# A decoder of six sublayers on one core: the mixture and the recurrence joined to the first attention, two norms in one factor

## The reference: what is computed

```python
x = _layernorm(x + _L0_attn_ref(x, ...))           # window attention, 16 heads; token 0 attends over all
x = _layernorm(x + _L0_xattn_ref(x, ctx_512, ...)) # causal attention plus cross attention, one output weight
x = _layernorm(x + _L0_ffn_ref(x, ...))            # mixture: each of 16 experts takes its 64 best tokens
x = _layernorm(x + _L1_attn_ref(x, ...))           # gated linear recurrence, then a gated MLP
x = _layernorm(x + _L1_xattn_ref(x, ctx_512, ctx_512, ...))
x = _layernorm(x + _L1_ffn_ref(x, ...))            # top 2 of 8 experts
```

## Time and profile before

| | us |
|---|---|
| median of three runs | 590.47 |
| lowest, highest | 588.93, 591.81 |
| the profiled execution | 588.99 |
| its span in the trace | 587.3 |
| first attention, to the last normed rows | 0 to 266.9 |
| mixture | 267.2 to 359.4 |
| recurrence and MLP | 359.9 to 417.8 |
| second attention with the top-2 mixture | 418.1 to the end |

### The profile page before, as it was taken

How to read it: one execution, slowest core, us unless ns; L and a number is a source line. 1 busy time by engine, 2 the same in 40 slices (tenths; PEclk the granted TensorE clock), 3 DMA queues, 4 the chain that set the end, 5 groups by cost and what they waited for, 6 DMA issues and landing times. The chain is left out here.

```text
span 587.3 us, 10442 instructions
## 1 busy us (share of the span) xinstructions
PE 478.7 (82%) x3790; PEld 233.6 (40%) x3837; DVE 381.4 (65%) x876; ACT 222.9 (38%) x449; POOL 181.0 (31%) x296
## 2 busy tenths in 40 slices
PE   3899999978879889875079994697599888999994
PEld 2445444433334333332037992246333333444441
DVE  7454766877667686515996557954458875466474
ACT  2303444454746646651002102432202666724221
POOL 6651639457363370406200004300142400000000
PEclk9899999999989999997589997989599999999998
DMA  7230103055411120006212004000031200060700
GB/s 233 67 81 27 47 2 103 19 172 173 138 55 27 49 56 4 3 1 226 98 53 93 3 2 160 1 2 1 26 89 48 57 3 3 33 184 1 215 19 18
DMA packets 26899, 38.03 MB, mean 65 GB/s; under 512 B 3648, under 2 KB 19520, under 8 KB 26464
## 3 DMA queue, kind: packets, MB, share of 16 engines
q1 hardware_dynamic: 26848, 37.36, 21.0%
HBM read 23.91 MB, written 0.59 MB: 42 GB/s over the span
## 5 line engine op out<-in xcount | busy, mean ns | idle before, releaser
L1070 DVE TENSOR_REDUCE nmax<-bank 128x2 f32<-128x512 f32 (+2 forms) x240 | 144.9, 625 | 79.8 <-PE bank L844 34.1
L956 ACT ACTIVATE arena<-bank 128x512 f32<-128x512 f32 (+2 forms) x256 | 130.7, 526 | 121.7 <-PE bank L848 84.4
L502 PE MATMUL bank<-causal_qk,identb 128*128 128x512 bf16 x255 | 80.8, 418 | 33.6 <-DVE moe_top L1350 16.0
L844 PE MATMUL bank<-arena 62*128 62x256 bf16 (+2 forms) x512 | 86.0, 257 | 12.9 <-DVE nmax L1070 5.3
L848 PE MATMUL bank<-arena 64*128 64x256 bf16 (+2 forms) x512 | 85.6, 256 | 2.2 <-ACT arena L956 1.5
L889 PE MATMUL bank<-arena 128*32 128x256 f32 (+4 forms) x1088 | 72.8, 346 | 8.6 <-ACT arena L956 3.7
L844 PEld LDWEIGHTS bank<-arena 62*128 62x128 bf16 x512 | 29.9, 94 | 79.3 <-issue 46.0
L502 PEld LDWEIGHTS bank<-causal_qk,identb 128*128 128x128 bf16 x298 | 26.4, 105 | 68.4 <-issue 40.0
L714 POOL TENSOR_SCALAR_AFFINE_SELECT arena<-arena 128x256 f32<-128x256 f32 x64 | 25.5, 407 | 48.6 <-ACT arena L956 47.8
L848 PEld LDWEIGHTS bank<-arena 64*128 64x128 bf16 x512 | 30.3, 94 | 16.5 <-issue 6.9
L889 PEld LDWEIGHTS bank<-arena 128*32 128x32 f32 x1088 | 21.4, 109 | 33.7 <-issue 18.6
(11 more groups left out here) (284 smaller groups left out, 794.5 us busy)
## 6 DMA issues: line engine op xcount, KB each, us to landing
arena<-arena SPq DMA_DIRECT2D x96, 128.0 KB, 2.4
fcw<-in_fc1T SPq DMA_DIRECT2D x16, 256.0 KB, 3.3
arena<-in_fc2T SPq DMA_DIRECT2D x1, 4096.0 KB, 14.9
arena<-comb_rows SPq DMA_DIRECT2D x16, 256.0 KB, 4.7
fcw<-in_last SPq DMA_DIRECT2D x1, 2304.0 KB, 8.3
arena<-pos_rows SPq DMA_DIRECT2D x16, 128.0 KB, 3.0
arena<-comb_rows SPq DMA_DIRECT2D x16, 128.0 KB, 4.5
w<-in_w SPq DMA_DIRECT2D x1, 1216.0 KB, 6.1
```

The source lines that it names most:

```text
L502: nc.tensor.matmul(bank[:, :], m.identb[:, :], m.causal_qk[:, 0:4, :], start=True, stop=True)
L844: mins = t.matmul(mout[:, i, :], stack_rows(m, nm, h0 + i, 0, MAX_ROWS)[:, qt * P:(qt + 1) * P], stack_rows(m, nm, h0 + i, 1, MAX_ROWS)[:, ...
L956: s.activation(m.prob[h % 8][:, 0:w], score_bank(n, h)[:, 0:w], ACT.Exp).then_inc(exps, 1)
L1070: v.tensor_reduce(m.nmax[n % 2][:, qt, h0:h0 + nh], MX[c % NMX][:, 0:nh * (k1 - k0)].rearrange("p (h k) -> p h k", h=nh), AX.X, ALU.max, n ...
```

## The change

Mixture and recurrence have no block of their own any more. `expert_choice` is now a side part of the first attention's pipeline and its `then`, which makes `LAST` the last job's table of steps instead of `FAR`; `recurrence` is called from it. The parts:

1. Every `cross` job that norms a sequence computes a second factor on GpSimd, (1 + eps) * var + 1e-5 * eps (`scaled_variance`), the power is taken for both at once (4 columns instead of 2), and DVE writes the rows twice: first as the mixture wants them (`m.x[1]`), then as before (`m.x[2]`). Squares, sums and the scaling of all rows at the mixture's start are gone.
2. Router, biases are loaded at slot 140, `fc2` behind the last value product. `norm_weight`'s transpose is at slot 226. Tiles 0 to 5 (three sequences) are transposed, weighed and multiplied by the router in slots 230 to 241, in the drain of the last job; only tiles 6 and 7 go through this chain after the last norm. GpSimd's constants are made at slot 230.
3. The scattered rows get x2 by 8 float32 matmuls with the identity, placed ahead of the scattering, in place of DVE's addition. Statistics and norms are made on pairs of tiles and read the banks. The norm's factor is that of layer norm and root mean square in one (`m.rms`); the rows with the layer norm alone, which the residual needs, are made from it on GpSimd (`rows_back`).
4. The large memset of the value buffers goes from DVE to GpSimd, the small ones behind the first `residual`.
5. The layer norm of tiles 4 to 7 at the end of the recurrence leaves the block: `LastNorm` makes it in the first slots of the second attention.
6. The `keep_warm` runs of 12 (mixture) and 8 (recurrence) matmuls are gone.

The core of the diff:

```diff
+def scaled_variance(nc, out, var, eps):
+    return nc.gpsimd.tensor_scalar(out, var, 1.0 + eps, LN_EPS * eps, ALU.mult, ALU.add)
...
                     pool.wait_ge(var_ready, i + 1)
+                    if n in scaled:
+                        scaled_variance(nc, m.veps[:, QT:2 * QT], m.mv[:, 0:QT, 1], MOE_EPS).then_inc(veps_ready, 1)
                     g.tensor_scalar(m.veps[:, 0:QT], m.mv[:, 0:QT, 1], LN_EPS, None, ALU.add).then_inc(veps_ready, 1)
...
-                    g.tensor_tensor(m.rstd[:, 0:QT], m.veps[:, 0:QT], m.eps[:, 0:1].broadcast_to([P, QT]),
+                    g.tensor_tensor(m.rstd[:, 0:w], m.veps[:, 0:w], m.eps[:, 0:1].broadcast_to([P, w]),
...
+                    if n in scaled:
+                        for q in range(QT):
+                            ins = v.tensor_scalar(m.x[1][:, QT * j.b + q, :], m.z[:, q, :], m.mv[:, q, 0:1],
+                                                  m.rstd[:, QT + q:QT + q + 1], ALU.subtract, ALU.mult)
+                        ins.then_inc(xs_ready, 1)
...
+GROUPS = ((0, 512), (512, 768), (768, 1024))
+S_ROUTER, S_NORM_COL, S_OPEN = 140, 226, 230
...
+    def tensor(pe, slot):
...
+        if slot == S_OPEN + 4:
+            pe.wait_ge(part.xs_ready, 3)
+            turned(pe, B[1], 4, range(4, 6), xnT_mm)
...
+    def tensor_on(pe):
+        t = nc.tensor
+        pe.wait_ge(part.xs_ready, 4)
+        turned(pe, B[3], 6, range(6, 8), xnT_mm)
+        routed(pe, B[1], 2)
...
-            keep_warm(nc, m, B[6], F_NORM)
...
+        for i in range(TILES):
+            t.matmul(out_rows(i), m.ident[:, :], x2[:, i, :], start=(i % 2 == 0), stop=False, skip_group_check=True)
+        scatter(0)
+        scatter(1)
+        rec.tensor_on(pe)
...
-                link(v.tensor_tensor(x2[:, ts, :], x2[:, ts, :], B[6 + c][:, :].rearrange("p (t d) -> p t d", d=D), ALU.add))
...
+        def norm_out(k):
+            dve.wait_ge(var_ready, k + 1)
+            dve.wait_ge(rms_ready, k + 1)
+            for i in (2 * k, 2 * k + 1):
+                ins = v.tensor_scalar(m.x[1][:, i, :], out_rows(i), m.mv[:, i, 0:1], m.rms[:, i:i + 1], ALU.subtract, ALU.mult)
+            if k % 2:
+                ins.then_inc(rec.xn_ready, 1)
...
+        rows_back()
+        stack_rest(nc, m, rest, 0)
+        g.memset(m.arena[:, 16384:20480], 0.0).then_inc(zeroed, 1)
...
-            keep_warm(nc, m, B[7], WARM)
...
+class LastNorm:
...
+    def gpsimd(self, pool, slot):
+        m = self.m
+        if slot == 1:
+            pool.wait_ge(self.var_ready, 1)
+            self.nc.gpsimd.tensor_tensor(m.rstd[:, 4:TILES], m.veps[:, 4:TILES], m.eps[:, 0:1].broadcast_to([P, 4]),
+                                         ALU.pow).then_inc(self.rstd_ready, 1)
...
+    def tensor(self, pe, slot):
+        m = self.m
+        if slot == S_NORMED:
+            pe.wait_ge(self.m1_read, self.m1_no["normed", 0])
+            pe.wait_ge(self.z_ready, 1)
+            for i in range(4):
+                ins = self.nc.tensor.transpose(m.bank[7][:, i * P:(i + 1) * P], m.x[1][:, 4 + i, :], m.ident[:, :])
+            ins.then_inc(self.m1_full, 1)
...
+    def vector(self, dve, slot):
...
+        if slot == S_SPLIT + 1:
+            dve.wait_ge(self.rstd_ready, 1)
+            for i in range(4, TILES):
+                link(v.tensor_scalar(m.x[1][:, i, :], xr[:, i, :], m.mv[:, i, 0:1], m.rstd[:, i:i + 1], ALU.subtract, ALU.mult))
+            v.sem_inc(self.z_ready, 1)
```

1225 lines of the change are left out of this document (648 added, 577 removed).

## The result

| us | before | with the change |
|---|---|---|
| median | 589.91 (4 runs) | 574.78 (4 runs) |
| lowest, highest | 588.93, 591.81 | 571.62, 576.76 |
| profiled execution | 588.99 | 571.62 |
| its span | 587.3 | 569.9 |

The ratio is 0.9726 with a 95% interval of 0.9697 to 0.9756: 2.7% faster. The forecast was 576.9 in a range of 570.8 to 583.0.

What follows compares the result with a forecast made beforehand. PE's products bound the attention bodies, a chain of single steps the block edges. 6.8 - 1.2 + 6.3 + 1.7 = 13.6 off 588.99 gives 575.4; with 1.5 to the median, 576.9, range 570.8 to 583.0.

Steps and rivals of the forecast that it cites:

- Step A: Routing behind the first attention's last norm: first `max` at 270.15 instead of 277.24, 7.1 saved, net 6.8 us.
- Additions in the attention: Extra rows and GpSimd work in the other three sequences' `cross` jobs: between 0 and 3.5 us, a third taken, -1.2.
- Steps B and C: From the scattering to the first scan: earlier projections 6.5, gates' input no longer waiting 1.2, clock -1.4; net 6.3 us.
- C's 1.2: Gates' first product: DVE came late because of its large memset; with that on GpSimd, 1.2 us gained.
- the clock's -1.4: Projections after the scattering: lower clock level expected for their first 2.5 us, costing 1.4 us.
- Step D: Recurrence's end: second attention starts 5.9 us earlier, 4.2 given back by late transposes ahead of the fill; net 1.7.
- R1: Whole kernel: everything is covered and the clock holds, 18.2 us gained, so 572.3; chance 0.22.
- R2: Additions paid in full: attention 2.3 more, drain 1.5 more, DVE slowed by GpSimd 1.0; 581.7; chance 0.20.
- R3: Second attention: clock stays low, its work takes twice as long, +15.4 us, 594.0 in all; chance 0.03.
- R4: Second attention's head: `LastNorm` is not covered at all and the whole 5.9 us is given back; 578.6; chance 0.06.
- R5: Drain: routing of tiles 0 to 5 isn't over at the last norm, half that gain lost; 580.3; chance 0.03.
- The rule weighed: New norms reading float32 from PSUM banks lack the faster mode: up to 0.3 us slower, sum 13.3.

Runs made afterwards that it cites:

- the first profile: Profiled execution (571.62 us) of the changed kernel's first measurement, against the kernel before; median 574.78 us, ratio 0.9726.
- the second profile: Profile from timing the changed kernel again, with no further edit, against the kernel before; 575.92 us, ratio 0.9771, profiled span 572.9.

## Why the prediction was right

It was right in the time (576.9 against 574.78, and 575.92 in the next measurement) and in the mechanism of the edges; inside the attention it was not, and part of the nearness of the sum is luck, as the last item shows. By its own steps:

- **Step A, 6.8.** Measured 12.98 - 6.22 = 6.76, less what the drain grew by, where I had taken 0.3: 0.13 from the last value product to the last statistics (6.14 before, 6.27 after), and 0.17 if the 8.4 us ahead of it are taken in, in which `norm_weight`'s transpose and four tiles' transposes stand. The dear parts were as priced: 1.04 for the power, 0.69 for two transposes, 1.04 for the router product (I had taken 1.04 with 0.1 on top of 0.94). The drain took the routing of tiles 0 to 5 with no more than that 0.17.
- **Additions in the attention, -1.2.** What failed here is the sentence that GpSimd's time "delays only the rows of a norm whose readers come much later": GpSimd's masks stand behind it, and TensorE waits for them 0.31 us ahead of a value product that comes 0.40 later. That is the one loss that every profile shows. VectorE's pair, of which I took a third, costs nothing from the second norm to the third (28.94 before and after); from the first to the second it is 34.94 to 35.83 against 35.17 in one profile before, so between a gain of 0.2 and a loss of 0.7 is open. With two pairs more, 0.86 of 1.2 was paid, so the cover is nearly used up there.
- **Steps B and C, 6.3.** The identity matmuls: 1.87 forecast, 1.87 measured, and 1.78 for a second set. Scattering's start to projection: 6.5 forecast net of them, 8.42 - 1.87 = 6.55 measured. C's 1.2 and the clock's -1.4 have to be taken together, because C only shows where the clock holds: the run with the memset on VectorE was no longer. Measured together they are 1.15 in the first profile and 0.5 in the second at the gates' first product, for -0.2 forecast. Of this less stays at the first MLP product: a gain of 0.39 in the first profile and a loss of 0.78 in the second, because the product beside GpSimd takes 0.30 more and the clock falls again behind it; with more fill it is a gain of 0.86. The -0.2 lies between them. What I had overlooked in C is B's own gain: the rows are ready at 352.44, 3.5 us ahead of the product's input, which is as long as the memset, though not as long as the memset with the 0.80 ahead of it.
- **The clock.** I looked at one place, the projections, and expected the lower level there. It was met in the second profile (3.6 at 0.61) and not in the first. A dearer place was not in the prediction: the MLP (13.79 at 0.78 in the second, 10.85 at 1.00 in the first, 12.54 before). Of the two, the second is the usual case: of the nine profiles of changed kernels with the old fills in these places six had 13.6 to 13.8.
- **Step D, 5.9 - 4.2 = 1.7.** The 5.9 was measured as 5.91. Given back were 4.06 in the first profile and 4.9 to 5.1 in the others with the transposes at slot 10, so D is worth 0.9 as a rule. The size of the fill behind them differs most (4.88 us in the first profile, 5.80 in the second, 5.2 forecast), which is the clock again. The mechanism (late transposes ahead of the fill) was right as far as it went, and moving them 8 slots brought 4.5 back. What I had wrong is what they wait for: I had named the norm's rows, which end at 404.37, but the bank that they fill is freed by L1017 behind those rows, at 405.14.
- **The sum.** It met the second profile's gain (14.4 for 13.6) with errors that cancel. What it had priced comes to some 12.75 there (6.6 - 0.4 + 5.8 + 0.75, the attention's open part left out). The MLP takes 1.25 that it had not, and the attention ahead of the third norm is 2.3 shorter, which no experiment ties to the change and which is within what the profiles of changed kernels differ by (4.2). The last 0.6 lie in the stretch ahead of the copy and in the one behind the first maximum.

**The rivals.** R1 (everything covered and the clock holds, 572.3) is near the first profile's execution, 571.62, but agrees with it in B and C alone (7.70 for 7.7); A was 6.6 instead of 7.6 and D 1.85 instead of 2.9, and a fast MLP and a shorter attention, which R1 did not hold, made up for them and for the slow gathering. R2 was to cost 4.8 more than the forecast, and the drain's 0.17 and the attention's 0.4 rule out most of it; its third term, VectorE slowed by GpSimd, came in part (0.30 in the gates' product). R3 did not come: the windows of the second attention show the clock at 1.00 from the first maximum on. The fill still stood directly before it, or, with the later transposes, before 0.5 us of idleness. R4 was nearer to the truth than its chance of 0.06 said: D gave back 5.1 of 5.9. R5 did not come.

**The rule weighed.** Rows from a bank take 0.70 a pair at 347.52 and 0.60 from SBUF at 266.25 in the first profile's times, so it is 0.05 more for each from a bank. The prediction's estimate was 0.07, from the Trainium skill (VectorE: DVE Perf Modes, "Why PSUM operands drop a tier"), by which float32 from PSUM has no faster mode; the trace agrees with its direction and nearly with its size.

## What to carry to other kernels

Work that is moved out of a chain into a later block has to be placed for each engine: the same transposes cost 4 to 5 us ahead of the warm-up matmuls and at most 0.7 eight slots later, with little else moved (their copy on ACT). Where a wait shows two conditions, look up what frees the bank as well as what makes the data before placing anything ahead of it. An engine that is idle for most of the time can still stand in the path: look for who waits for the next instruction in its queue (GpSimd's masks here). And when the spread of executions is as large as the effect, compare stretches between two events: most of those in which the clock doesn't fall came back within 0.03 us in thirteen profiles, while whole times of one kernel moved by up to 9.

## What the runs showed that I had not expected

**The clock falls in different places in executions of one kernel.** Two profiles of the changed kernel had it fall in different stretches, at the cost of 1.7 us in the gathering and 2.9 in the MLP. The six runs of the changed kernel spread over 6.9 us (574.18 to 581.05), and those with more `keep_warm` and the late transposes over 2.2 (566.19 to 568.40). That more fill narrows the spread isn't shown by this: the group of the second was narrower in the kernel before too, six runs with the same fills and the early identity matmuls spread over 5.1 (565.53 to 570.60), and five with the old fills over 2.8 (573.69 to 576.48).

**GpSimd slows VectorE in some operations and not in others.** In the first profile VectorE's remainder of the split took 1.21 us at 401.02, beside GpSimd's L705 at 400.82, and 0.68 in the kernel before without it:

```profile
423.24 0.68 DVE L976 TENSOR_TENSOR rem<-qk,arena 128x512 f32<-128x512 f32 x1
```

In the run with the later transposes four `tensor_scalar` took 2.71 instead of 1.49, beside GpSimd's split at 407.92, with one of the four at 1.23 (the other rows stand in the timelines of the head above).

These are more cases like the earlier trace rows. The product of 512 columns at 355.93 took 0.99 beside GpSimd's multiplication (354.34) and 0.69 beside its memset. So the price of moving work to GpSimd is paid on VectorE, in the operations that happen to run beside it, and depends on what GpSimd does. The Trainium skill (GPSIMD Engine Reference, "Key points") says that the two share interfaces to SBUF; these rows agree with it for GpSimd's operations that read rows in SBUF; beside the memset, which reads nothing, no slowing shows.
